# A cross-attention kernel: the order in which score maxima, scores and value sums follow each other on TensorE, and a shorter warm-up

## The reference, cut to what matters

```
q = (query @ Wq + bq)            # 128 x 256, 16 heads
k = (key_value @ Wk + bk)        # 12544 x 256
v = (key_value @ Wv + bv)
attn = softmax(einsum('bhqd,bhkd->bhqk', q, k) * scale)
x = einsum('bhqk,bhkd->bqhd', attn, v) @ Wo + bo
```

## Time and profile before

| | |
|---|---|
| median of 3 runs | 1280.26 us (1278.75 to 1282.37) |
| profiled execution, its own time | 1283.87 us |
| its span | 1282.0 us |
| PE busy / DVE busy / ACT busy | 1140.0 / 712.5 / 704.9 us |
| POOL busy | 202.1 us |
| mean granted clock of PE | 0.975 |
| L0 attention, about | 3.9 to 520 us |
| L1 attention, about | 687 to 1198 us |

### The profile page before, as it was taken

The page is one execution under the profiler, slowest core; times in us unless marked ns, Lnnn a source line. Parts: engine busy times, 40 slices in busy tenths (PEclk is TensorE's granted clock), DMA queues, the critical chain, the costliest instruction groups (busy, mean ns, idle before and its releaser), DMA issues.

```text
span 1282.0 us, 30469 instructions
## 1 busy us (share of the span) xinstructions
PE 1140.0 (89%) x13011; PEld 735.0 (57%) x13011; DVE 712.5 (56%) x1356; ACT 704.9 (55%) x1387; POOL 202.1 (16%) x114
## 2 busy tenths in 40 slices
PE   8899999999999999716799899999999999999777
PEld 5455555565555565516696455555555555565565
DVE  3665555556556564489323676556555565565343
ACT  4476566666666666442213466666666565566422
POOL 0231221222212110000000222122222111210000
PEclk9999999999999999858999999999999999999889
DMA  9664434444434350440822854444343344350360
GB/s 205 143 152 109 110 95 116 116 100 104 103 91 105 88 171 3 145 152 1 308 79 60 186 138 105 106 116 115 89 116 92 92 116 103 84 147 2 141 213 5
DMA packets 84248, 144.92 MB, mean 113 GB/s; under 512 B 10056, under 2 KB 73936, under 8 KB 83600
## 3 DMA queue, kind: packets, MB, share of 16 engines
q1 hardware_dynamic: 83216, 142.85, 42.7%
q10 hardware_dynamic: 896, 0.12, 0.1%
HBM read 64.64 MB, written 0.15 MB: 51 GB/s over the span
## 4 chain that ended last, share of the span: by engine, by line
PE 57%; DVE 24%; ACT 10%; issue 5%; DMA 2%; SPq 2%; DVEq 0%; ACTq 0%
PE ring L583 28%; DVE mpart L1317 16%; PE st L583 13%; PE ot L583 12%; ACT work L1053 6%; SPq L406 2%; DVE arena L1456 1%; PE ring L750 1%; ACT arena L1018 1%; DMA warena<-ctxT 1%; ACT arena L1029 1%; ACT work L1059 1%; DMA arena<-rows 1%; PE ring L711 1%; DVE arena L1436 1%
## 5 line engine op out<-in xcount | busy, mean ns | idle before, releaser
L1317 DVE TENSOR_REDUCE mpart<-ring 128x1 f32<-128x448 f32 x896 | 518.8, 620 | 370.0 <-PE ring L583 364.2
L1053 ACT ACTIVATE work<-st 128x512 f32<-128x512 f32 x784 | 404.6, 606 | 100.6 <-PE st L583 99.2
L583 PE MATMUL ring<-arena,qst 96*128 96x448 bf16 x896 | 267.4, 357 | 14.9 <-DVE mpart L1317 11.1
L583 PE MATMUL ot<-work,arena 128*17 128x128 f32 x6272 | 232.1, 275 | 9.4 <-ACT work L1053 0.6
L583 PE MATMUL st<-qst,arena 97*128 97x128 bf16 x3136 | 238.2, 219 | 1.1 <-DMA qst<-rowb 1.1
L583 PEld LDWEIGHTS st<-qst,arena 97*128 97x128 bf16 x3136 | 190.8, 98 | 59.3 <-issue 41.0
L544 POOL TENSOR_TENSOR arena<-arena 128x896 f32<-128x896 f32 x52 | 98.0, 1884 | 629.5 <-ACT arena L1025 629.3
L583 PEld LDWEIGHTS ot<-work,arena 128*17 128x17 f32 x6272 | 144.6, 97 | 79.4 <-ACT work L1053 46.1
L583 PEld LDWEIGHTS ring<-arena,qst 96*128 96x128 bf16 x896 | 79.1, 98 | 140.8 <-DVE mpart L1317 88.2
L583 PE MATMUL ring<-wkv,warena 64*128 64x256 f32 (+1 forms) x640 | 130.0, 400 | 12.1 <-DVE mpart L1317 12.1
L583 PE MATMUL ring<-warena,wkv 64*128 64x448 f32 (+1 forms) x352 | 119.8, 576 | 11.9 <-DVE mpart L1317 11.9
(11 more groups left out here) (284 smaller groups left out, 767.9 us busy)
## 6 DMA issues: line engine op xcount, KB each, us to landing
arena<-arena SPq DMA_DIRECT2D x336, 224.0 KB, 3.8
arena<-ffn_W SPq DMA_DIRECT2D x16, 1024.0 KB, 13.1
warena<-ctxT SPq DMA_DIRECT2D x60, 224.0 KB, 4.6
warena<-ctxT SPq DMA_DIRECT2D x26, 448.0 KB, 4.0
arena<-f SPq DMA_DIRECT2D x2, 4096.0 KB, 26.3
arena<-scratch_bc SPq DMA_DIRECT2D x1, 2048.0 KB, 7.2
arena<-rows SPq DMA_DIRECT2D x1, 1792.0 KB, 6.9
wkv<-L_wkv SPq DMA_DIRECT2D x8, 128.0 KB, 5.7
```

The lines of the kernel that those rows point to most:

```text
L583: return nc.tensor.matmul(o, l, r, start=start, stop=stop, **kw)
L1053: nc.scalar.activation(pbuf[:, n % 2, half * 512:(half + 1) * 512], st[:, 2 * (n % 2) + half], ACT.Exp).then_inc(*signal(f"{lay}_exp_done"))
L1317: V.reduce_max(mpart[:, 2 * h + hf:2 * h + hf + 1], ring[:, BANKS[step][0], 0:HALF], AX_X).then_inc(*signal(f"{lay}_b_max"))
```

## The change

Four edits, all of order but for the first:

1. `WARM` from (16, 2) to (6, 2): ten identity multiplications fewer at the start of `L0`.
2. In each pair, one maximum now stands between the value sums and the first scores, one stands between the two scores (as before), and one maximum fewer stands behind the second scores. The number in a pair stays (`n`).
3. In chunks 12 and 13 the value sums are single units: pv, scores, pv, scores, where it was pv, pv, scores, scores.
4. In the prologue the maxima of chunk 0 come in threes between single `k` and `v` steps, where it was fours, twos and a burst of eight; `row` of chunk 0 now stands behind the four `v` steps of chunk 2, and behind it stand four maxima of chunk 1, scores 0, one, scores 1, two.

```diff
-WARM = (16, 2)
+WARM = (6, 2)
...
-    plan += pair("v", 0, 0) + pair("v", 0, 2) + pair("k", 1, 0) + pair("k", 1, 2) + [("k1", 1, 0)] + some(4, 0)
-    plan += [("v", 1, 0), ("k1", 1, 1)] + some(2, 0) + [("v", 1, 1), ("k2", 1, 0)] + some(4, 0)
-    plan += [("v", 1, 2)] + some(2, 0) + [("v", 1, 3), ("k2", 1, 1)] + some(4, 0)
-    plan += [("k", 2, 0)] + some(2, 0) + [("k", 2, 1)] + some(4, 0)
-    plan += [("k", 2, 2)] + some(2, 0) + [("k", 2, 3)] + some(8, 0)
-    plan += pair("v", 2, 0) + [("row", 0, 0)] + pair("v", 2, 2) + some(2, 1) + score(0) + some(2, 1) + score(1)
-    plan += some(3, 1)
+    plan += pair("v", 0, 0) + pair("v", 0, 2) + pair("k", 1, 0) + pair("k", 1, 2) + [("k1", 1, 0)]
+    plan += some(3, 0) + [("v", 1, 0), ("k1", 1, 1)] + some(3, 0) + [("v", 1, 1), ("k2", 1, 0)]
+    plan += some(3, 0) + [("v", 1, 2)] + some(3, 0) + [("v", 1, 3), ("k2", 1, 1)]
+    for kind, k in (("k", 0), ("k", 2), ("v", 0)):
+        plan += some(3, 0) + [(kind, 2, k)] + some(3, 0) + [(kind, 2, k + 1)]
+    plan += some(2, 0) + pair("v", 2, 2) + [("row", 0, 0)]
+    plan += some(4, 1) + score(0) + some(1, 1) + score(1) + some(2, 1)
...
-            plan += [("pv", c, 2 * w), ("pv", c, 2 * w + 1)]
-            if w == UNITS // 2 - 1:
-                plan.append(("ot", c, 0))
+            sums = [("pv", c, 2 * w), ("pv", c, 2 * w + 1)] + [("ot", c, 0)] * (w == UNITS // 2 - 1)
+            single = c >= NCH - 2
+            plan += sums[:1] if single else sums
...
-            plan += score(c * UNITS + 2 * w + 2) + some(1, limit) + score(c * UNITS + 2 * w + 3)
-            plan += some(n - 1 - made, limit)
+            plan += some(1, limit) + score(c * UNITS + 2 * w + 2) + (sums[1:] if single else [])
+            plan += some(1, limit) + score(c * UNITS + 2 * w + 3)
+            plan += some(n - 2 - made, limit)
```

## The result

The changed kernel takes 1219.42 us (median of 4 runs, 1214.53 to 1221.23) against 1280.89: a ratio of 0.9515, 95% interval 0.9483 to 0.9548. The forecast was 1223, range 1212 to 1246. The profiled execution has a span of 1218.7, 63.3 less than the earlier trace rows.

A forecast was written before the change was run, and what follows sets the result against it. PE was taken as the bound, held up once a pair by its own burst of maxima. Terms 40.8 + 4.1 + 3.4 + 6.2 + 1.0 + 1.6 + 0.7 + 0.3 = 58.1 us less gave 1223, range 1212 to 1246.

The forecast's parts named there:

- The wait of a pair: Pairs with a ring step behind: value sums to f32 step falls from 3.17 to 2.77, 0.40 us less.
- One chunk: Chunks 1 to 10: 2.04 us less each, period 35.49 to 33.45, 40.8 us over ten chunks and two layers.
- An f32 step 0.29 behind a maximum: End of a pair's burst: a maximum's matmul takes 0.29 where an f32 step follows, against 0.19 otherwise.
- Nothing waits: Pair in the spread order: maximum 4 and the f32 step find their banks free, at 2.48 and 2.77.
- The loop of w = 4: Pair w = 4, only the row behind it: scores to scores binds at 3.16, 3.38 becomes 3.16, 0.22 less.
- Single units: Last pairs of a layer: single units break the loop of 2.96, a pair takes 2.46; 3.1 a layer, 6.2 us.
- a single unit with its exit is 1.11 - 0.45 = 0.66: Scores in the last pairs: sixteen units' matmuls and exit 1.11, eight without exit 0.45, so one unit with exit 0.66.
- The clock and the prologue: Prologue: threes of maxima keep PE at work, no clock fall near 50 us; 1.6 us less in L0, 0.7 in L1.
- Dearer passages: Rival, chance 0.17: leaving value sums for a maximum costs 0.10 more, single units' changes as much; about 1242.
- ACT's chain in more pairs: Rival, chance 0.06: ACT's copies delay exponentials in w = 0 and 5 too, losing 0.80 a chunk; about 1241.
- No change: Rival, chance 0.02: PE's stall is not the ring but something that keeps the pair's length; 1280.
- Later scores making it slower: Rival, chance 0.03: the maximum ahead of the scores delays every exponential by 0.19 in all seven pairs; about 1306.

The follow-up runs named there:

- The shorter maxima: Kernel before the change, each maximum taken over 224 of its 448 columns and queries scaled down by 256, order unchanged: 1241.31 us.
- the late `k2`: Changed kernel with ACT's copy k2 of keys' part 0 moved from the end of w = 5 to the end of w = 6: 1210.29 us, ratio 0.946.
- the last kernel: Changed kernel with k2 moved behind w = 6's exponentials and two maxima ahead of the first scores in w = 0, 2, 3, 5: 1204.54 us, ratio 0.9387.

## Why the prediction was right, and where it was not

- **The wait of a pair: right.** 3.17 became 2.72, forecast 2.77. The shorter maxima moved the wait by exactly the difference of DVE's durations. The 0.10 that I feared for the passage from value sums to a maximum isn't there: 1.00 (228.07 - 227.07).
- **One chunk: 2.04 forecast, 2.23 measured**, over ten chunks and two layers 40.8 against 44.6. Two small terms were wrong. "An f32 step 0.29 behind a maximum" was too high: two maxima and the transposition take 0.43, and 0.38 without waiting, so the last costs 0.19 like any. The 0.29 had been read ahead of value sums, where it holds. "Nothing waits" was wrong by 0.05 a pair. That makes 0.45 and 0.46 in w = 1 and 3 instead of 0.40. The loop of w = 4 was sized rightly: 3.15 from scores to scores (243.06 to 246.21), forecast 3.16.
- **Single units: the mechanism was right, the term was mis-sized.** 3.1 a layer forecast, 4.9 measured. The step that failed is "a single unit with its exit is 1.11 - 0.45 = 0.66": it is 0.55 (473.15 to 473.70), and a pair 2.23, not 2.46, which over eight loops is the missing 1.8. The 1.11 held no exit but a wait for DVE, as the shorter maxima showed (0.90). So the passage out of scores that the prediction put at 0.21 is 0.10, and only where value sums follow. Chunk 12's share was forecast at 1.0 and was 0.5: in L1 single units take back half of what the spread order gives there, and in L0 PE waits for the row's DMA, 2.17 instead of 1.10:

```profile
476.01 0.62 PE L583 MATMUL st<-qst,arena 97*128 97x128 bf16 x8 [1.10 <-DMA qst<-rowb]
```
```profile
448.89 0.62 PE L584 MATMUL st<-qst,arena 97*128 97x128 bf16 x8 [2.17 <-DMA qst<-rowb]
```

- **The clock and the prologue: the sign was right, the reason wrong.** The clock stayed full near 50 us, as forecast, but fell at 55.14 in L0 and at 703.68 in L1, just behind the prologue, where PE waits for row and v copies. From row 0 to row 1 it took 26.2 and 26.4, where the kernels with single units in w = 0 and with the late `k2`, whose order there is the same, had no fall at that place and took 24.9 to 25.2: the fall cost some 1.2 a layer. In prologues and chunk 0 the forecast was 6.7 for all and the trace gives 6.0 without, 5.9 with the stretch that holds L1's prologue.
- **The warm-up: nothing**, as measured alone; the forecast was 0.3 between -1.6 and 0.75.
- **The rivals.** Dearer passages: not so. ACT's chain in more pairs: not so, w = 0 and 5 kept their gain. No change: ruled out by the shorter maxima. Later scores making it slower: true only of short pairs, 0.2 to 0.3 each.
- **The sum: 58.1 forecast, 61.5 between the medians, 63.3 between the profiles.** That it came so close is in part luck. The steady chunks gave 3.8, the single units 3.6 and chunk 11 0.2 more than forecast; chunk 12, prologues and chunk 0, and the stretches outside the attentions gave 2.4 less.

## What to carry to other kernels

Where one engine fills a small ring of banks and another empties it, count back from each step to the one whose bank it takes: a burst as long as the ring makes the step behind it wait for the burst's first element, though the emptying engine is idle most of the time. Spread such steps between others, but put what a third engine's chain needs first in the pairs that are short, and the bank waits' cure in those that are long. Alternating two kinds of matmul costs a tenth of a microsecond each way here; it pays only where PE has a stall to fill, which the timeline shows as a stretched entry and the list of waits does not.

## What the runs showed of the hardware that was not expected

A change of kind costs PE time only into and out of value sums. Into them it is 0.10: a maximum takes 0.29 ahead of value sums (226.78 to 227.07) and 0.19 otherwise, eight matmuls of scores 0.55 (473.15 to 473.70) instead of 0.45. Out of them it is some 0.12: eight groups take 1.00 and four 0.57 (473.70 to 474.27), so a group is 0.11, and 0.12 to 0.13 is left. From bf16 to f32 work without value sums it is nothing: sixteen matmuls of scores take 0.90 ahead of the f32 transposition `o` (505.09 to 505.99 before) and ahead of the f32 `row` (469.93 to 470.83 in the kernel with shorter maxima). Value sums are the ones that lie in column tiles; that this is the reason no run here shows.

The clock's fall in the prologue of L0 came at a different place in each profile, or not at all, in kernels whose orders differ little there: beginning between 37 and 41 us in four of the fourteen profiles, at 49.66 before, at 55.14 (just behind it) after, and nowhere up to 70 us in the other eight. It moves a single execution by 1 to 2 us, which is about what the intervals of the prologue's and the warm-up's runs can tell.

The faster chunks brought a longer stall. At the first scores of chunk 12 in L0 PE waits 1.85 to 2.2 for the row's DMA in each of the nine kernels with the spread order, and 2.16 in the one with the old order and shorter maxima, against 1.1 to 1.5 in the four others. In seven of the nine the clock fell to 0.50 at most 1.5 us from that stall's end, and the stretch from row 12 to row 13 took 24.7 to 26.7; in the two without a fall it took 24.0 (the changed kernel) and 24.3. So it is in the last kernel (timeline of PE, and a window):

```profile
440.15 0.92 PE L585 MATMUL st<-qst,arena 97*128 97x128 bf16 x8 [2.00 <-DMA qst<-rowb]
```
```profile
440.30:443.70 3.40, 3.40 (x35) 2.21 (x33) 1.62 (x3) 2.17 (x4) 0.00 (x0) 0.50 0.02 5
```

No run here took this stall away; why the row's DMA lands late there stays open.
